# A four-layer attention and expert kernel: gates applied inside the expert loops, and each tile's second weights copied to a fixed buffer

## The reference, cut to what matters

```python
# f0: 8 experts, the best one of each token counts
weights = softmax(top2(flat @ Wr));  out = weights[:, 0] * (gelu(flat @ W1[e1]) @ W2[e1])
# f1: 8 experts, the best two; e1, e2 and their gates p1 + p2 = 1
out = p1 * (gelu(x @ w1[e1] + b1[e1]) @ w2[e1] + b2[e1]) + p2 * (the same with e2)
# f2: 16 experts; each expert takes its own C = 512 best tokens ("expert choice")
scores = softmax(flat @ gate_w.T).T;  w, idx = top_k(scores, 512)
out[idx] += w * ((gelu(x[idx] @ Wg.T) * (x[idx] @ Wu.T)) @ Wd.T);  out += a shared expert
# f3: 8 experts, the best two by a small two-layer router; as f1, with relu in place of gelu
```

## Time and profile before

| | us |
|---|---|
| device time, median of 3 runs (lowest, highest) | 1689.83 (1685.56, 1692.47) |
| device time of the profiled execution | 1689.31 |
| span of its profile | 1687.5 |
| PE busy | 1147.7 (68%) |
| DVE busy | 793.7 (47%) |
| ACT busy | 617.0 (37%) |
| POOL busy | 840.8 (50%) |

### The profile page before, as it was taken

One profiled execution on the slowest core, in us unless ns is written; L12 is line 12 of the kernel. 1 busy time (PEld: TensorE's weight loads), 2 busy tenths in 40 slices (PEclk: granted clock), 3 DMA queues, 4 the chain that ended last, 5 costly groups with the idle time before them and its releaser, 6 DMA issues. The chain is left out here.

```text
span 1687.5 us, 30101 instructions
## 1 busy us (share of the span) xinstructions
PE 1147.7 (68%) x8612; PEld 905.0 (54%) x8613; DVE 793.7 (47%) x2043; ACT 617.0 (37%) x1219; POOL 840.8 (50%) x944
## 2 busy tenths in 40 slices
PE   3547744892766777436767789937999785667771
PEld 2436742682566766425434455524788534666761
DVE  4550017467822322288873432335899536222223
ACT  2124435341344444354221122214454532444443
POOL 6136637464156555462435768835444102555554
PEclk9669877996889888868978999979999985998886
DMA  3051125000411111211212445540000013111114
GB/s 106 2 165 42 42 72 106 3 0 7 163 35 40 37 40 39 67 63 49 55 50 65 81 91 101 118 72 6 1 0 0 8 65 113 39 39 41 39 39 159
DMA packets 87352, 95.54 MB, mean 57 GB/s; under 512 B 19509, under 2 KB 66742, under 8 KB 86774
## 3 DMA queue, kind: packets, MB, share of 16 engines
q1 hardware_dynamic: 63974, 59.90, 12.0%
q0 software_dynamic: 22848, 32.67, 8.7%
q10 hardware_dynamic: 464, 2.16, 0.3%
HBM read 65.53 MB, written 29.16 MB: 56 GB/s over the span
## 5 line engine op out<-in xcount | busy, mean ns | idle before, releaser
L981 PE MATMUL psum<-f_xsT,f_w1e 128*128 128x128 f32 x1448 | 235.5, 315 | 152.5 <-issue 95.6
L981 PEld LDWEIGHTS psum<-f_xsT,f_w1e 128*128 128x128 f32 x1448 | 210.3, 223 | 170.0 <-issue 146.9
L952 POOL DMA_INDIRECT d_y<-f_y,f_dst x181 | 178.3, 985 | 191.7 <-DVE f_y L1075 131.4
L948 POOL DMA_INDIRECT f_xs<-d_xn,f_src x181 | 175.3, 969 | 139.3 <-SPq L944 85.0
L1060 DVE TENSOR_TENSOR f_hpre<-psum,f_b 128x512 f32<-128x512 f32 x142 | 98.2, 691 | 260.5 <-remote 93.5
L989 PE MATMUL psum<-f_w,f_hT 128*128 x1448 | 210.5, 294 | 2.8 <-ACT f_hT L1030 2.8
L989 PEld LDWEIGHTS psum<-f_w,f_hT 128*128 128x128 f32 x1448 | 196.3, 211 | 3.2 <-issue 3.2
L488 PE MATMUL psum<-ident,xn 128*128 128x128 f32 x256 | 47.8, 363 | 173.2 <-DVE xn L461 172.9
L1015 ACT COPY f_w1e<-f_w 128x512 f32 x184 | 113.7, 618 | 66.5 <-PEq L1665 30.4
L488 PEld LDWEIGHTS psum<-ident,xn 128*128 128x128 f32 x256 | 40.6, 189 | 179.4 <-ACT xn L502 173.9
L1030 ACT ACTIVATE f_hT<-f_hpre 128x512 f32<-128x512 f32 x142 | 89.5, 630 | 111.9 <-DVE f_hpre L1060 90.6
(11 more groups left out here) (462 smaller groups left out, 2356.9 us busy)
## 6 DMA issues: line engine op xcount, KB each, us to landing
f_yback<-d_y SPq DMA_DIRECT2D x20, 512.0 KB, 6.5
d_xn<-xn SPq DMA_DIRECT2D x3, 2048.0 KB, 7.6
...
a_v<-in_ctx SPq DMA_DIRECT2D x4, 1024.0 KB, 7.9
...
f_xs<-d_xn,f_src POOLq DMA_INDIRECT x181
```

Of the source, the lines that this page charges most:

```text
L948: nc.gpsimd.indirect_dma_start(xs[:, u % RX, :], None, k.d_xn, bass.IndirectOffsetOnAxis(m.src[:, n:n + 1], 0)).then_inc(gathered[u % RX], 16)
L952: nc.gpsimd.indirect_dma_start(k.d_y, bass.IndirectOffsetOnAxis(m.dst[:, n:n + 1], 0), y[:, u % RT, :], None).then_inc(scattered[u % RT], 16)
L981: last = nc.tensor.matmul(BH[u % 2][:, s * P:(s + 1) * P], w1e[:, u % RT, s * P:(s + 1) * P], xsT[:, u % 2, :], start=True, stop=True)
```

## The change

**Gates.** The rows of `d_xn` become 130 numbers long. Column 128 holds the gate of the token's first choice, column 129 the second gate minus the first. The store of `xn` moves from the head of SyncE's queue to ScalarE's, behind the gates. A new table `m.second` says for each slot whether it is a second choice. The separate block that turned the biases goes: the transposition joins route's TensorE list and the copy its VectorE list.

```diff
-self.xn = self.sb("xn", [P, NT, D])
+self.xn_rows = self.sb("xn", [P, NT, GROW])
+self.xn = self.xn_rows[:, :, 0:D]
...
-sp.dma_start(k.d_xn[0:T, :].rearrange("(p j) d -> p j d", p=P), k.xn[:]).then_inc(xst, 16)
...
 dve.wait_ge(exd, 1)
-step(TS(m.gate[:, 0, :], m.gate[:, 1, :], 1.0, None, ALU.add))
-step(nc.vector.reciprocal(m.gate[:, 0, :], m.gate[:, 0, :]))
-step(TT(m.gate[:, 1, :], m.gate[:, 1, :], m.gate[:, 0, :], ALU.mult))
+of_first, to_second = k.xn_rows[:, :, D], k.xn_rows[:, :, D + 1]
+step(TS(gate[:, 0, :], gate[:, 1, :], 1.0, None, ALU.add))
+step(nc.vector.reciprocal(of_first, gate[:, 0, :]))
+step(TT(gate[:, 1, :], gate[:, 1, :], of_first, ALU.mult))
+TT(to_second, gate[:, 1, :], of_first, ALU.subtract).then_inc(gates_made, 1)
...
+step(TS(m.second[:], tile_i[:], float(NT), None, ALU.is_ge))
...
+if m.b1 is not None:
+    dve.wait_ge(b1_turned, 1)
+    step(nc.vector.tensor_copy(m.b1[:], k.bank[7][:, 0:NE * HS]))
...
-nc.scalar.activation(m.gate[:, 1, :], mx[:, 3, :], ACT.Exp).then_inc(exd, 1)
+nc.scalar.activation(gate[:, 1, :], mx[:, 3, :], ACT.Exp).then_inc(exd, 1)
+act.wait_ge(gates_made, 1)
+act.dma_start(k.d_xn[0:T, :].rearrange("(p j) d -> p j d", p=P), k.xn_rows[:]).then_inc(xst, 16)
...
+if m.b1 is not None:
+    pe.wait_ge(wl, 16 * len(weights))
+    nc.tensor.transpose(k.bank[7][:, 0:NE * HS], m.b1_rows[:], k.ident[0:NE * HS, 0:NE * HS]).then_inc(b1_turned, 1)
```

```diff
-xs = sb("xs", [P, RX, D])
+xs = sb("xs", [P, RX, GROW])
+slot_gate = sb("slot_gate", [P, RX])
...
+w2e = sb("w2e", [P, RT, FF])
...
+wait(pool, gate_kept, n - RX + 1)
...
-wait(pool, x_turned, n + AHEAD - RX + 1)
+wait(pool, gate_kept, n + AHEAD - RX + 1)
...
-def expert_of(n):
-    return pe.value_load(m.expert[0:1, bass.ds(n, 1)], min_val=0, max_val=NE - 1)
...
+def down_proj(n, u):
+    pe.wait_ge(w2_copied, n + 1)
     pe.wait_ge(activated, n + 1)
     wait(pe, y_ready, n - 1)
     for s in range(HS):
-        last = nc.tensor.matmul(BY[u % 2][:, 0:D], hT[:, u % RT, s, :], m.w2[:, bass.ds(e * FF + s * D, D)],
+        last = nc.tensor.matmul(BY[u % 2][:, 0:D], hT[:, u % RT, s, :], w2e[:, u % RT, s * D:(s + 1) * D],
                                 start=s == 0, stop=s == HS - 1)
...
-e = expert_of(n)
...
-down_proj(n, u, e)
...
+def copy_w2(n, u, e):
+    wait(dve, down, n - RT + 1)
+    nc.vector.tensor_copy(w2e[:, u % RT, :], m.w2[:, bass.ds(e * FF, FF)]).then_inc(w2_copied, 1)
+def keep_gate(n, u):
+    dve.wait_ge(x_turned, n + 1)
+    wait(dve, y_ready, n - RX + 1)
+    row, at = xs[:, u % RX], slot_gate[:, u % RX:u % RX + 1]
+    if m.choices == 1:
+        nc.vector.tensor_scalar(at, row[:, D:D + 1], 1.0, None, ALU.mult).then_inc(gate_kept, 1)
+    else:
+        nc.vector.scalar_tensor_tensor(out=at, in0=row[:, D + 1:D + 2], scalar=m.second[:, bass.ds(n, 1)],
+                                       in1=row[:, D:D + 1], op0=ALU.mult, op1=ALU.add).then_inc(gate_kept, 1)
...
 def body(i, turn=RX, end=False):
-    es = [expert_of(RX * i), expert_of(RX * i + 1)] if m.b1 is not None else []
+    es = [expert_of(RX * i), expert_of(RX * i + 1)]
     for u in range(turn):
         n = RX * i + u
-        if m.b1 is not None and (not end or u + 2 < turn):
+        if not end or u + 3 < turn:
+            keep_gate(n + 3, u + 3)
+        if not end or u + 2 < turn:
             es.append(expert_of(n + 2))
-            bias(n + 2, u + 2, es[u + 2])
+            if m.b1 is not None:
+                bias(n + 2, u + 2, es[u + 2])
+            copy_w2(n + 2, u + 2, es[u + 2])
         dve.wait_ge(down, n + 1)
         wait(dve, scattered[u % RT], 16 * (RX // RT) * i + 16 * (u // RT))
-        if m.b2 is None:
-            nc.vector.tensor_copy(y[:, u % RT, :], BY[u % 2][:, 0:D]).then_inc(y_ready, 1)
-        else:
-            nc.vector.tensor_tensor(y[:, u % RT, :], BY[u % 2][:, 0:D], m.b2[:, bass.ds(es[u] * D, D)],
-                                    ALU.add).then_inc(y_ready, 1)
-if m.b1 is not None:
-    bias(0, 0, expert_of(0))
-    bias(1, 1, expert_of(1))
...
+        src = BY[u % 2][:, 0:D]
+        if m.b2 is not None:
+            nc.vector.tensor_tensor(y_sum[:, u % RT, :], src, m.b2[:, bass.ds(es[u] * D, D)], ALU.add).then_inc(y_summed, 1)
+            dve.wait_ge(y_summed, n + 1)
+            src = y_sum[:, u % RT, :]
+        dve.wait_ge(gate_kept, n + 1)
+        nc.vector.tensor_scalar(y[:, u % RT, :], src, slot_gate[:, u:u + 1], None, ALU.mult).then_inc(y_ready, 1)
+for n in range(3):
+    keep_gate(n, n)
+for n in range(2):
+    e = expert_of(n)
+    copy_w2(n, n, e)
+    if m.b1 is not None:
+        bias(n, n, e)
```

```diff
+def add(eng, c, q):
+    eng.wait_ge(back[c][q], 16)
+    xs = flat(k.x[:, tiles(q), :])
+    return eng.tensor_tensor(xs, flat(y[:, c, q]), xs, ALU.add)
+def by_pool(q):
+    return m.choices == 2 or q % 2 == 1
...
-@block.scalar
-def _(act):
-    for q in range(PARTS):
-        act.wait_ge(back[0][q], 16)
-        for t in range(TP):
-            j = q * TP + t
-            last = nc.scalar.activation(y[:, 0, q, t, :], y[:, 0, q, t, :], ACT.Identity, scale=m.gate[:, 0, j:j + 1])
-        last.then_inc(scaled, 1)
...
-pool.wait_ge(scaled, q + 1)
-if m.choices == 2:
-    pool.wait_ge(second, q + 1)
-xs = flat(k.x[:, tiles(q), :])
-nc.gpsimd.tensor_tensor(xs, flat(y[:, 0, q]), xs, ALU.add).then_inc(summed, 1)
+if by_pool(q):
+    add(nc.gpsimd, m.choices - 1, q).then_inc(second, 1)
...
-dve.wait_ge(back[1][q], 16)
-for t in range(TP):
-    j = q * TP + t
-    last = nc.vector.scalar_tensor_tensor(out=k.x[:, j, :], in0=y[:, 1, q, t, :], scalar=m.gate[:, 1, j:j + 1],
-                                          in1=k.x[:, j, :], op0=ALU.mult, op1=ALU.add)
-last.then_inc(second, 1)
...
-    dve.wait_ge(summed, q + 1)
+    if m.choices == 1 and by_pool(q):
+        dve.wait_ge(second, sum(by_pool(c) for c in range(q + 1)))
+    else:
+        dve.wait_ge(summed, sum(m.choices == 2 or not by_pool(c) for c in range(q + 1)))
     for t in range(TP):
         tile_stats(k, q * TP + t)
 for q in range(PARTS):
     if m.choices == 2:
-        add_second(q)
+        dve.wait_ge(second, q + 1)
+    if m.choices == 2 or not by_pool(q):
+        add(nc.vector, 0, q).then_inc(summed, 1)
```

```diff
+def rank(n):
+    es = slice(n * EG, (n + 1) * EG)
+    pe.wait_ge(gt_ready, n + 1)
+    nc.tensor.matmul(k.bank[5][:, RANKS], trim[:], flat(gt[:, es]), start=True, stop=False)
+    nc.tensor.matmul(k.bank[5][:, RANKS], onesb[:], flat(gt_sum[:, es]), start=False, stop=True).then_inc(gt_ranked, 1)
+    pe.wait_ge(eq_ready, n + 1)
+    nc.tensor.matmul(k.bank[7][:, RANKS], trim[:], flat(eq[:, es]), start=True, stop=False)
+    nc.tensor.matmul(k.bank[7][:, RANKS], onesb[:], flat(eq_sum[:, es]), start=False, stop=False)
+    nc.tensor.matmul(k.bank[7][:, RANKS], onesb[:], bc(gt_sum[:, es, NT - 1], (P, EG, NT), 2), start=False, stop=True).then_inc(eq_ranked, 1)
+rank(0)
...
-    invert(group, 2 * u)
+if group and u == 0:
+    rank(group)
+if group and u:
+    invert(group, 1)
...
-    if group:
-        invert(group, 2 * u + 1)
+    if group and u == 0:
+        invert(group, 0)
 if group:
+    invert(group, 2)
+    invert(group, 3)
     place(group)
...
+if i:
+    step(TT(thr[:], thr[:], took[:], ALU.bitwise_or))
...
-    step(TT(thr[:], thr[:], took[:], ALU.bitwise_or))
+step(TT(thr[:], thr[:], took[:], ALU.bitwise_or))
...
+def mark(n, flag, total_, op, ready):
+    es = slice(n * EG, (n + 1) * EG)
+    step(TT(flag[:, es].rearrange("p e j -> p j e"), sc[:, :, es], bc(thr_bc[:, es], (P, NT, EG), 1), op))
+    nc.vector.tensor_tensor_scan(flat(total_[:, es]), flat(seg[:, es]), flat(flag[:, es]), 0.0, ALU.mult, ALU.add).then_inc(ready, 1)
...
+def slot_digits(n):
+    es = slice(n * EG, (n + 1) * EG)
+    dve.wait_ge(gt_ranked, n + 1)
+    step(STT(out=flat(s1[:]), in0=k.bank[5][:, RANKS], scalar=-1024.0, in1=flat(gt[:, es]), op0=ALU.add, op1=ALU.mult))
+    dve.wait_ge(eq_ranked, n + 1)
...
+mark_greater(0)
+mark_equal(0)
+slot_digits(0)
...
-    if group:
-        (lo_hots, hi_hots)[s % 2](group, 2 * u + s // 2)
+    if group and u == 0 and s < 2:
+        (mark_greater, mark_equal)[s](group)
+    if group and u:
+        (lo_hots, hi_hots)[s % 2](group, 1 + s // 2)
+if group and u == 0:
+    slot_digits(group)
+if group:
+    lo_hots(group, 3 * u)
+    hi_hots(group, 3 * u)
```

91 lines of the change are left out of this document (36 added, 55 removed).

## The result

The kernel after took 1729.95 us (median of four runs, 1721.14 to 1735.69), the kernel before 1687.69 on the same chip: a ratio of 1.0237, with a 95% interval of 1.0204 to 1.0269. The change made the kernel 2.4% slower; 1.4% faster was forecast. The profiled execution took 1728.13 us.

The account below looks back on a forecast made before the run. With late signals gone, VectorE's serial chain was taken to bound f1 and f3. Terms: +7 f1/f3, -9 f0, -13.5 combines, +0.5 route, -9 f2 = -24, so 1689 - 24 = 1665 us, range 1605 to 1730.

Parts of the forecast that it names:

- the late signals: Expert loops: VectorE starts up to 3 us after TensorE's recorded end; blamed on TensorE's register loads, forecast to vanish.
- VectorE's chain: f1 and f3: VectorE's serial work per tile becomes the bound, 3.28 us against 3.25 before; +7 us with the prologue.
- the start of the loops: f1 and f3: longer prologue, three gates kept and two copies before the first bias, +1.5 us in each.
- f0: First expert loop: tile falls from 2.92 to 2.66 us, -10 us over 38 tiles, +1 for the prologue.
- the head: f1 and f3: two more register loads and the branch every four tiles on VectorE, 1.8 us, 0.45 a tile.
- the port's 0.1: f1 and f3: VectorE's new operations slowed by a port shared with POOL, 0.1 us a tile.
- Combines: Combines of f0, f1, f3: scaling goes, additions split between POOL and VectorE; -4.5, -5 and -4, sum -13.5 us.
- f2: Stage f2: only group 0 of the experts before the first one-hot, OR moved behind the counts; sum -9 us.
- C: Rival for f1 and f3: late signals are not due to TensorE's register loads and stay; 1723 us, chance 0.16.
- D: Rival: VectorE's two-port work and POOL exclude each other for whole instructions in the expert loops; 1788 us, chance 0.09.

Follow-up runs that it names:

- e7: The kernel after with the expert-tile loops written out on TensorE and VectorE, VectorE keeping registers and loading one a tile: 1679.35 us, 0.987 of before.
- e15: The kernel before without the expert loops' scatters and with only the first four gathers of each loop: 1504.72 us, 0.884 of before.
- e3: The kernel before with TensorE's loop over the expert tiles written out, register loads kept, where no late signals stood: 1548.27 us, 0.999 of before.
- e18: The kernel after, unchanged, run where no late signals stood in the expert loops: 1622.19 us, 1.047 of before.
- e5: The kernel before, unchanged, run again where late signals stood: 1698.88 us, a single run.
- e6: The kernel after, unchanged, run again where late signals stood: 1755.42 us, 1.033 of before.
- group 2: Follow-up runs on one chip with late signals, beside the kernel before, which took 1697.72 us there.
- e11: The kernel before with f2 alone as in after: 1542.24 us, 0.993 of before.
- e4: The kernel after without the copy of the second weights, TensorE loading its register again and the gates kept in the loops: 1567.18 us, 1.011 of before.

## Why the prediction was wrong

**The step that failed** is "I let the late signals vanish". It rested on TensorE's register loads as the cause ("likely, not shown"). After has no such load and keeps the signals, 15 late copies in each of f1 and f3 for 13 and 15 in before; e7 has neither load nor branch and keeps them; e15 has the loads and loses them with POOL's DMAs. The same reasoning had made say too much: a load stands in every tile, and so beside every stall.

**What that did to the sum.** The forecast set VectorE's chain of 3.28 us a tile against a tile of 3.25 and found a draw. But those 3.25 are POOL's pace and the stalls, while the 3.28 had no stalls in it. So the stalls had been taken out of after and left in before. With e3 and e18 the tile can be split, in f1 and f3 (us a tile, 70 from first scatter to last):

| | loop without stalls | stalls | sum |
|---|---|---|---|
| before | 2.47, 2.47 (e3) | 0.73, 0.75 | 3.20, 3.22 |
| after, forecast | 3.28 | 0 | 3.28 |
| after | 3.06, 3.02 (e18) | 0.50, 0.49 | 3.57, 3.52 |

In after the stalls cost 70 us in the two loops that the forecast put at nothing. The loops e3 and e18 are of other groups than the first traces, which is why e5 and e6, both of group 2, count as a second case: there the stalls cost 0.79 and 0.80 us a tile in before and 0.71 and 0.72 in after. VectorE's longer chain does not make the stalls dearer; they cost somewhat less beside it. It costs its own 42 and 39 us where nothing is late, and of that 26 and 21 are left in the first traces, 36 and 33 in group 2. The loop of before, for all its idle time, makes up for next to nothing: its stalls cost 51 and 53 us for 44 and 55 us of lateness.

From 1665 to the measured 1728 are 63 us: 70 for the stalls in f1 and f3, -33 for a chain counted too long, 5 and 2 for the tile of before and the start of the loops, 13 for f0 and 6 for the other stages.

**The chain itself** was counted well, somewhat high: 2.67 for 2.77, the head 0.44 for 0.45 a tile, and the port's 0.1 did not come; 3.11 in place of 3.28, and 3.04 with the quicker end of the loops. Over 140 tiles that is the 33 us. (PE's busy share in the three loops, read as 72 to 76%, is 71 to 76 in the earlier trace rows; nothing hangs on it.) The single durations fit (429 ns for 0.43, 284 and 288 for 0.29).

**f0**: 9 us less were forecast, 4.1 more came. Of the 10 that the late signals were to give nothing came; the gate and the copy together cost 2.7 us in e18 against e3 (92.6 and 89.9).

**The start of the loops**: 1.5 us each for f1 and f3, measured 3.1 and 1.9. The longer prologue's instructions were counted, not what the gate of tile 2 waits for with tile 0's bias behind it.

**Combines**: -13.5 forecast. f0's stretch gave 3.1 for 4.5, f3's 3.6 for 4. f1's combine, from the last scatter to VectorE's last statistics, went from 30.8 to 28.0, so 2.8 for 5: the scaling is gone, but the two engines that now add at once slow each other.

**f2**: -9 forecast; 7.9 are left of the 10.7 when f1's combine is taken off. The stretch to the one-hots gave 10.1 where 9.2 were forecast; that the groups in the bodies took some back is likely and not shown. e11 shows a gain of 0.7% (0.5 to 1.0) for this part alone.

**Rivals.** C came, with 0.16: the late signals stay. Its 1723 is 5 us from the profiled 1728, but partly by luck: it put the stalls of f1 and f3 at 48 us, which were 70, and kept the chain that was 33 too long. Its reason, that the stalls weigh because VectorE has no slack any more, is not what the runs show, as they cost no more in after than in before. And it need not have taken a third of the 0.69 us to undo the gain: f0's 10 us lost, 14 over 138 tiles are 0.10, a seventh. Of D nothing came in the loops. The copies of after:

```profile
L1081 DVE COPY f_w2e<-f_w x181: 416/418/629, 118.6 to 1694.1; 128x512 f32 x181
```

At least half take 418 ns or less. The 76 that lie wholly inside one of POOL's indirect DMA instructions take 418 in the median, as the 78 that touch none; of the 27 that run over the end or the start of one the median is 475. So no lock for a whole instruction is seen there. In the combine it is: VectorE's addition that starts at 751.69, just behind POOL's of 751.62 to 754.01, ends 1.09 us behind that one, after 3.42 us in place of 1.23. The Trainium skill (SBUF — State Buffer, Who interferes with whom) says that a VectorE instruction with two inputs in SBUF contends with a GpSimd instruction that reads SBUF, and that the shared pair is an exclusive lock. The trace agrees for POOL's arithmetic; for its indirect DMAs beside VectorE's copies it shows no such lock.

**Open**: why late signals stand in some groups and not in others, whether the gathers or the scatters bring them, and whether TensorE's work or only its signal is late. It is not the loading of code: of all the instruction packets in before's trace three start in f1's loop (at 490, 492 and 667 us), which has 13 late copies, and three in f3's (at 1439, 1548 and 1653), which has 15. The gates' price apart from the copy was measured only where nothing is late (e4: 1.1% above before, f2 and the combines included).
